# One transformer kernel on one core: ends of the walk merged, shifted copies moved to ScalarE, engine orders written anew

## The chip, the cores and the metric

The kernel runs on one core of a Trainium2 chip. The metric is the device time of that core in microseconds (us), from start to end of one execution, on fixed inputs. A core has five engines with a queue of instructions each: TensorE (PE, matrix products into eight PSUM banks), VectorE (DVE), ScalarE (ACT), GpSimd (POOL), and SyncE (SP), which here only issues DMAs. The queues run side by side; semaphores are all that orders them against each other, and inside a queue everything runs in the order in which it was written.

## The reference, cut to what matters

The input is `x`, 8 batches of 512 tokens of width 128, fp32. Everything after the input is done per batch, and no batch needs another.

```python
xn = layernorm(x)
x  = x + delta_rule_attention(xn)      # 4 heads of 128 / 32, a recurrence over the 512 tokens
       + local_stack(xn)               # 2 layers: windowed attention, then a gated MLP
xn = layernorm(x)
x  = x + latent_attention(xn)          # 16 heads of 8, causal softmax over all 512 keys
       + mixture_of_experts(xn)        # 6 experts, top 2 of 6, and a shared one

def shift_token(t):                    # used twice in each layer of local_stack
    t1, t2 = split(t, 2, axis=-1)
    t2 = pad(t2, one row in front)[:, :-1]
    return concatenate([t1, t2], axis=-1)

def layer(x):                          # of local_stack
    h = shift_token(x); q, k, v = split(h @ wqkv, 3)
    q = rotary(l2norm(q) * qs); k = rotary(l2norm(k) * ks)
    x = x + attention_in_windows_of_64_with_one_back(q, k, v) @ wo
    h = layernorm(shift_token(x)) * lg + lb
    a, g = split(h @ w1 + b1, 2)
    return x + (a * gelu(g)) @ w2 + b2
```

## The kernel before, in words

The weights stay in SBUF. A batch's tokens are four chunks of 128. Between the layers of the local stack the activations lie transposed, channels on partitions and tokens along the free axis (`xnT`, `hT`, `r1T`, `h2T`), so that `shift_token` is two copies: partitions 0 to 63 as they are, partitions 64 to 127 one column to the right (`shifted`, L1405 to L1407, run by DVE). It is called at `hcopy` (head norm to `hT`, the input of layer 0), at `fres` of both layers (`r1T` to `h2T`, before the MLP's layer norm, with a memset of the first column), and at the end of `fw2` of layer 0 (to `hT`, the input of layer 1). `hT_` (L1421) copies the transposed head norm from PSUM to `xnT`, on DVE as well.

The work of a batch is cut into seven streams of steps, one letter each. `f`: head norm, and the chunks' q, k, v products, rotation (`fqk`), norm (`frs`, `fscale`) and transposes (`fqT`, `fkT`). `b`: for each layer and chunk scores (`fS`), softmax (`fnorm`), transposes (`fPT`), values (`fPV`), output product (`fwo`); then the MLP (`fres`, `fln`, `fapply`, `hnT`, `fg`, `gelu`, `fa`, `fw2`); at the end `x1`, which adds the three parts, its layer norm (`x1_apply`), and its transposes (`xn2T`). `e`: the delta rule's keys, their gram blocks (`gram`), and `solve`, which inverts 16 x 16 diagonal blocks in 15 pairs of dependent DVE instructions, after the gram blocks have gone to DRAM and the diagonal has come back. `d`: the delta rule itself, a block inversion (`inv_v`, `inv_zx`) and a recurrence over chunks (`seq_*`), ending in `delta_back`, `delta_norm` and `oT0`. `m`: latent attention's projections (`lat`, `mq`, `rope`, `split`, `left`, `send`) and the experts (`eu`, `ew`, `e_down`). `a`: the pass that finds the maxima of the scores (`mS`, `mrow`). `c`: the pass with exponentials and values (`mST`, `mPV`, `matg`), ending in `aT` and `final`, which writes the batch out.

`walk` (L278) writes each engine's queue. It goes over periods; in period p there are `f`, `b` and `d` of batch p, `e` of batch p+1, and `m`, `a`, `c` of batch p-1. Period -1 holds only the head, two chunks of `f` and `e` of batch 0, and period 8 only `m`, `a`, `c` of batch 7. Inside a period each engine takes one step of the stream that the next letter of its string in `ORDER` names:

```python
    for p in range(-1, BATCH + 1):
        left = {s: collections.deque(x for x in steps if x[0] in parts) for s, steps in period(p).items()}
        for s in ORDER[engine][0 if p < 0 else 1 if p == 0 else p - BATCH + 4 if p >= BATCH - 1 else 2]:
            if left[s]:
                name, *at = left[s].popleft()
                parts[name](*at)
```

So there are five strings per engine: for period -1, 0, 1 to 6 (the steady one), 7 and 8. Nothing of a period can be written into a queue before all of the period ahead of it has been. The strings are data: they fix every order among steps that no dependency fixes. In the steady one, DVE's `solve` stands between the MLP's last gated product (`fa`) and `fw2` of layer 1.

Of the kernel before, what the change touches and what calls it, by code (L numbers as in the profile page):

```python
# [42 lines left out]
         "fefefeefeffffefeeeeeee"),  # L43
        (
         "bdfdfdddfbfdbbddbdfddbddfddfbbfbddbdddfdfdbdddffdbdebdbddbddbddddddddddbddbdbdbbddddbdbdbbbbbdbffdfeffefeffefb"
         "effbebebefbfffebeefebbfbebfbffbffbbbbfffbbfbfbbbbbbbbfbbbb"),
        (
         "dddddmbdmfddfbddbmbfddbffddbdfdddfdbdbfdbfdfmdbdddmdbdmdfdmfbddmdbbdbeddbddmddmddbmbdddmdbdmdbddbmddmdbmbbbabb"
         "abmabmafafmaaffaafmdfaffamabmafafmcabcbfcabfacbccfamacfcabacmcafcmafacbbcmcabcfabccaefaceacbceacafcafbcabecabc"
         "aeccabcfacbceacfccafeabcaeacbecfaccabaebcfcaecabccfcafcfcececcbccbcbbbbbcccbcccccccbccccb"),  # L50
        (
         "dddddmbdmfddfmbdbdfddbfbddfdbdfdfddddmbdbdfdbdddmdbdmdfddmddddfmfdbddmddfdmbdbdbdbdbdmddbdbmbdmbdmdbmmabmababb"
         "abmababdabmafamfafaaffamfacffacmacbcamccafafcbabmbcafccabcamccaffcmbcamacffaccbbacbcfcfcacabcafabcfafccabcabac"
         "bcabacbccaacabcabcabccabacaccbcaccacccbcbbcbbbbcbccbcccccbccccccccc"),
# [1964 lines left out]
```

## Time and profile before

| | |
|---|---|
| three runs, median (lowest to highest) | 2007.26 us (2005.38 to 2016.96) |
| the profiled execution's own time | 2011.66 us |
| its span, first to last instruction | 2009.9 us |
| instructions | 43996 |
| granted TensorE clock, mean | 0.949 of full |
| busy: PE, DVE, ACT, POOL | 1749.7, 1344.0, 938.6, 816.9 us |

Busy time is the time in which an engine had at least one instruction under way; issuing DMAs and waiting on semaphores is not counted. An engine's idle time is named after what released it. Line numbers are those of the kernel before. The clock is given as the share of full speed that was granted: 1.00 is 2.4 GHz, 0.50 is 1.2 GHz, and a value between is a mean over both. Where PE runs at 0.50, its instructions take up to twice as long and count as busy all the same.

### The profile page before, as it was taken

Reading aid. Unit: us, or ns where it says so; the run is one execution under the profiler, and the core shown is the slowest. Engines: PE = TensorE matmul, PEld = TensorE weight load, DVE = VectorE, ACT = ScalarE, POOL = GpSimd, SP = SyncE. Lnnn points to the kernel's source line nnn. Section 1 sums busy time; section 2 is a strip of 40 time slices with the busy share of each in tenths; the row PEclk is TensorE's granted clock in tenths of the full one; section 3 lists DMA queues with packets and bytes.
Section 4 is the critical chain, followed back from the end, with each engine's and each line's share of the span. In section 5 each row is a group of like instructions: output and inputs, shape, how many; then the busy total and the mean of one; then the engine's idle time right before and its main releaser. Section 6 shows DMA issues by size and latency. Waiting matters only on the chain.

```text
span 2009.9 us, 43996 instructions
## 1 busy us (share of the span) xinstructions
PE 1749.7 (87%) x16664; PEld 1136.1 (57%) x16664; DVE 1344.0 (67%) x3602; ACT 938.6 (47%) x2473; POOL 816.9 (41%) x819
## 2 busy tenths in 40 slices
PE   2597769998899979999899979999899989988787
PEld 1474537655674647655575647656575646745343
DVE  2464547776777767776678767787677766675373
ACT  1243434375434745366344745356443754345323
POOL 2434635364335625265235534175145534253000
PEclk9699889999899999999899999999899999999787
DMA  4210112201112022201122012201122011210020
GB/s 178 63 31 12 32 40 62 54 13 38 43 55 60 11 48 74 58 18 38 36 62 60 10 38 70 73 17 36 38 62 60 10 38 51 64 29 15 13 74 6
DMA packets 126625, 89.91 MB, mean 45 GB/s; under 512 B 42168, under 2 KB 113976, under 8 KB 126136
## 3 DMA queue, kind: packets, MB, share of 16 engines
q1 hardware_dynamic: 126128, 86.44, 16.0%
q8 instruction: 133, 2.18, 0.4%
q10 hardware_dynamic: 288, 0.67, 0.1%
q14 instruction: 76, 0.62, 0.1%
HBM read 46.84 MB, written 25.17 MB: 36 GB/s over the span
## 4 chain that ended last, share of the span: by engine, by line
PE 51%; DVE 16%; issue 8%; POOL 8%; ACT 6%; DVEq 0%; ACTq 0%; POOLq 0%
PE bank L691 7%; PE bank L1083 3%; PE bank L1069 3%; ACT shared L1333 2%; PE bank L798 2%; PE bank L832 2%; PE bank L824 2%; PE bank L1068 2%; PE bank L837 2%; PE bank L808 2%; POOL qk_rs L1790 2%; PE bank L1041 2%; PE bank L721 2%; POOL soft L1829 2%; DVE rot L1450 2%
## 5 line engine op out<-in xcount | busy, mean ns | idle before, releaser
L1829 POOL TENSOR_TENSOR soft<-soft,prec 128x512 f32<-128x512 f32 x128 | 137.3, 1082 | 442.4 <-DVE prec L1468 442.4
L1333 ACT ACTIVATE shared<-bank 128x512 f32<-128x512 f32 (+1 forms) x384 | 201.1, 528 | 240.5 <-PE bank L1069 238.8
L1637 DVE TENSOR_REDUCE nmx<-bank 128x1 f32<-128x512 f32 (+3 forms) x352 | 223.2, 637 | 128.2 <-PE bank L1041 125.8
L1243 ACT ACTIVATE soft<-bank,nmax 128x128 f32<-128x128 f32 x512 | 180.1, 382 | 101.4 <-DVE nmax L1460 100.5
L1790 POOL TENSOR_TENSOR qk_rs<-qk_rs,minus_half 128x16 f32<-128x16 f32 x64 | 187.7, 2932 | 5.3
L721 PE MATMUL bank<-w_sb,hT 128*128 128x512 f32 x256 | 138.0, 625 | 11.8 <-DVE hT L1407 6.0
L1068 PE MATMUL bank<-b_sb 128*128 128x128 bf16 x512 | 115.5, 227 | 34.7 <-ACT shared L1333 34.3
L1069 PE MATMUL bank<-shared 75*128 75x384 bf16 (+3 forms) x512 | 144.7, 310 | 0.0
L1788 POOL TENSOR_SCALAR rs_f<-mv_f 128x4 f32<-128x4 f32 x24 | 5.7, 236 | 325.8 <-DVE mv_f L1396 325.8
L1041 PE MATMUL bank<-shared 72*128 72x256 bf16 (+3 forms) x512 | 127.1, 300 | 0.0
L691 PE MATMUL bank<-c_sb,soft 128*128 128x128 f32 x608 | 100.1, 291 | 26.5 <-DVE soft L1402 12.9
L1207 ACT ACTIVATE rot<-bank 128x512 f32<-128x512 f32 x128 | 78.8, 616 | 92.1 <-PE bank L721 91.8
L1243 ACT ACTIVATION_READ_ACCUMULATOR soft<-bank,nmax 128x1 f32 x512 | 113.5, 222 | 0.0
L1068 PEld LDWEIGHTS bank<-b_sb 128*128 128x128 bf16 x512 | 49.2, 99 | 109.4 <-ACT shared L1333 74.5
L1252 ACT ACTIVATE soft<-bank 128x512 f32<-128x512 f32 x128 | 77.7, 608 | 69.7 <-PE bank L691 69.1
L1083 PE MATMUL bank<-shared,vaug 128*32 128x512 f32 (+3 forms) x1024 | 94.5, 466 | 9.8 <-ACT shared L1333 9.7
L1038 PE MATMUL bank<-b_sb 128*128 128x128 bf16 (+2 forms) x352 | 86.6, 246 | 17.2 <-DVE nmx L1637 15.0
L691 PEld LDWEIGHTS bank<-c_sb,soft 128*128 128x128 f32 x608 | 70.8, 148 | 53.9 <-POOL soft L1829 29.4
L1460 DVE TENSOR_REDUCE nmax<-bank 128x4 f32<-128x512 f32 x128 | 82.2, 683 | 28.1 <-PE bank L778 27.6
L1443 DVE TENSOR_REDUCE qk_ss<-rot 128x8 f32<-128x512 f32 x128 | 86.5, 676 | 11.0 <-ACT rot L1207 10.6
L727 PE MATMUL bank<-w_sb,hT 128*128 128x512 f32 x128 | 69.2, 623 | 15.7 <-DVE rot L1450 15.7
L1806 POOL TENSOR_TENSOR k_f<-k_f,rot 128x256 f32<-128x256 f32 x64 | 48.5, 757 | 70.4 <-DVE rot L1450 70.3
(250 smaller groups left out, 4503.0 us busy)
## 6 DMA issues: line engine op xcount, KB each, us to landing
shared<-parts_dram SPq DMA_DIRECT2D x64, 288.0 KB
vm<-v_f SPq DMA_DIRECT2D x112, 128.0 KB, 2.4
parts_dram<-parts SPq DMA_DIRECT2D x96, 128.0 KB, 2.4
L_dram<-the SPq DMA_DIRECT2D x32, 256.0 KB, 2.3
shared<-X_dram SPq DMA_DIRECT2D x32, 256.0 KB, 3.1
shared<-L_dram SPq DMA_DIRECT2D x32, 256.0 KB, 3.8
w_sb<-weights SPq DMA_DIRECT2D x1, 4167.0 KB, 19.4
x_tm<-x SPq DMA_DIRECT2D x8, 256.0 KB, 5.2
```

Of the source, the lines that this page charges most:

```text
L691: m = nc.tensor.transpose(ps[0:width, i * P:(i + 1) * P], src(i), ident)
L721: mm(place(("fq", "fk")[i], c)[:], hT[:, c * P:(c + 1) * P], W(f"wqkv{l}")[:, i * T:(i + 1) * T], start=True, stop=True).then_inc(fk_psum ...
L1038: mm(ps[:, :, c * P:w], B("identb"), repeat(B("causal"), len(heads)), start=True, stop=False, skip_group_check=True)
L1041: m = mm(ps[:, i], Qst[0:9 * DM, h * T + c * P:h * T + w], Kst[0:9 * DM, h * T:h * T + w], start=False, stop=True, skip_group_check=True)
L1068: mm(ps[:, at:at + P], B("identb"), B("causalT"), start=w == 0, stop=False, skip_group_check=True)
L1069: m = mm(ps[:, at:at + wide], Kst[0:9 * DM + 3, h * T + j * P:h * T + (j + 1) * P], Qst[0:9 * DM + 3, h * T + j * P:(h + 1) * T], start=Fa ...
L1083: m = mm(place("mPV")[VW * i:VW * (i + 1), j * P:T], vaug[:, at_v:at_v + VW], v4(PTm, 2, GROUP)[:, n % 2, i, at:at + wide], start=j == 0, ...
L1243: a = af(v4(p_sb, 2, 4)[:, j, g], place("fS", j)[:, g * P:(g + 1) * P], ACT.Exp, bias=nmax[:, at:at + 1], accum_out=psums[:, at:at + 1])
L1333: af(v4(PTm, 2, GROUP)[:, u % 2, i, 0:n], place("mST", b, i)[:, 0:n], ACT.Exp).then_inc(mexp_done, 1)
L1637: reduce(v3(nmx[:], HM)[:, h:h + len(heads), c], v3(place("mS", b, t)[:, 0:len(heads) * (c + 1) * P], len(heads)), AX, ALU.max, negate=Tru ...
L1790: return tt(dst, dst, minus_half[:, 0:dst.shape[1]], ALU.pow)
L1829: tt(p, p, spread(prec[:, at:at + NPAIR], P), ALU.mult).then_inc(fnorm_done, 1)
```

## The change

Three edits. First, periods -1 and 0 become one, and so do 7 and 8: `period(0)` is the old one of -1 with that of 0 behind it, stream by stream, `period(7)` likewise. There are now four strings per engine: for period 0, 1 to 5, 6, and 7. Steps of either old part may be written between steps of the other, as far as one stream's order allows. Second, `hT_`, `hcopy`, `shifted`, and with it the copies of `fres` and of `fw2` of layer 0, are run by ACT. DVE keeps the memset in `fres` and signals it separately, so that PE's `fln` waits for two signals per layer (one by DVE, one by ACT). Third, all strings are new. The computation is the same.

```diff
@@ period, walk
 def period(p):
 
+    if p == 0 or p == LAST:
+        one, two = (part(q) for q in ((-1, 0) if p == 0 else (LAST, BATCH)))
+        return {s: one[s] + two[s] for s in STREAMS}
+    return part(p)
+
+
+def part(p):
+
     if p < 0:
...
-    for p in range(-1, BATCH + 1):
+    for p in range(BATCH):
         left = {s: collections.deque(x for x in steps if x[0] in parts) for s, steps in period(p).items()}
-        for s in ORDER[engine][0 if p < 0 else 1 if p == 0 else p - BATCH + 4 if p >= BATCH - 1 else 2]:
+        for s in ORDER[engine][0 if p == 0 else p - BATCH + 4 if p >= BATCH - 2 else 1]:
@@ TensorE
                 def fln(b, l):
-                    pe.wait_ge(h2_done, ly(b, l) + 1)
+                    pe.wait_ge(h2_done, 2 * ly(b, l) + 2)
@@ ScalarE
+                def shifted(dst, src):
+                    af(dst[0:64, :], src[0:64, :], ACT.Copy)
+                    return af(dst[64:P, 1:T], src[64:P, 0:T - 1], ACT.Copy)
+
+                def hT_(b):
+                    act.wait_ge(head_psum, b + 1)
+                    if b:
+                        act.wait_ge(P_psum, NT * b)
+                        act.wait_ge(r1_done, ch(b - 1, 1, 0))
+                    af(xnT[:], place("hT")[:], ACT.Copy).then_inc(head_copied, 1)
+
+                def hcopy(b):
+                    act.wait_ge(head_copied, b + 1)
+                    if b:
+                        act.wait_ge(fv_psum, ch(b, 0, 0))
+                    shifted(hT, xnT).then_inc(hT_copied, 1)
...
+                def fres(b, l):
+                    act.wait_ge(r1_done, ch(b, l, NT))
+                    if l:
+                        act.wait_ge(h_done, b + 1)
+                    elif b:
+                        act.wait_ge(x1_psum, b)
+                    shifted(h2T, r1T).then_inc(h2_done, 1)
+
+                def fw2(b, l):
+                    if l == 0:
+                        act.wait_ge(r_done, ly(b, l) + 1)
+                        act.wait_ge(fv_psum, ch(b, 1, 0))
+                        shifted(hT, r2T).then_inc(h_done, 1)
@@ VectorE (hT_, hcopy and shifted go)
                 def fres(b, l):
-                    dve.wait_ge(r1_done, ch(b, l, NT))
                     if l:
                         dve.wait_ge(h_done, b + 1)
                     elif b:
                         dve.wait_ge(x1_psum, b)
-                    nc.vector.memset(h2T[64:P, 0:1], 0.0)
-                    shifted(h2T, r1T).then_inc(h2_done, 1)
+                    nc.vector.memset(h2T[64:P, 0:1], 0.0).then_inc(h2_done, 1)
...
                     stt(r2T[:], place("fw2")[:], W(f"cols{l}")[:, 6:7], r1T[:], ALU.add, ALU.add).then_inc(r_done, 1)
-                    if l == 0:
-                        dve.wait_ge(r_done, ly(b, l) + 1)
-                        dve.wait_ge(fv_psum, ch(b, 1, 0))
-                        shifted(hT, r2T).then_inc(h_done, 1)
```

What the strings mean where the prediction speaks of them, written out as steps (batch, layer, chunk as numbers; `|` is where a period ended):

```text
DVE, start.   before: k.0.3, fqk.0.0.1, beta, gram.0, gram.1, gram.2, gram.3, solve.0 | fS.0.0.0, bg, fqk.0.0.2, fnorm ...
              after:  k.0.3, fqk.0.0.1, beta, bg, gram.0, gram.1, fS.0.0.0, gram.2, fnorm.0.0.0 (both), gram.3,
                      fqk.0.0.2 (both), fwo.0.0.0, solve.0, fS.0.0.1, fqk.0.0.3 ...
PE, start.    before: hT.0, k.0.0, fqk.0.0.0 ... kT.0 to kT.3, gram.0 to gram.3 | fS.0.0.0, qT.0.0 ... qT.0.3, bg, fv.0.0.2 ...
              after:  hT.0, k.0.0, qT.0.0, k.0.1, fqk.0.0.0 ... bg, kT.0 to kT.3, gram.0, fqT.0, fkT.0, gram.1, fS.0.0.0,
                      gram.2, fqk.0.0.2 (both), gram.3, fPT (both), fv.0.0.2, fPV, fwo.0.0.0, fqT.1, fkT.1, fqk.0.0.3 (both),
                      fS.0.0.1, fv.0.0.3, fPT.0.0.1 (both), fqT.2, then the first inv_v
ACT, start.   after:  hT.0, k.0.0, hcopy.0, qT.0.0, k.0.1, fqk.0.0.0 ...
SP, start.    before: ... gram.0.3, solve.0, fv.0.0.0, fv.0.0.1, keep.0 | x_load.1, inv_load.0.0 ...
              after:  ... gram.0.3, fv.0.0.1, solve.0, fv.0.0.2, keep.0, x_load.1, inv_load.0.0 ...
ACT, layer 0's MLP in the steady string.
              before: ... seq_u.3, seq_o.3, gelu, eu.3, delta_back, fqk.1.0 ... (oT0 after fkT.1.0)
              after:  ... seq_u.2, fres, seq_o.2, ... seq_u.3, seq_o.3, delta_back, hT (of the next batch), gelu, fw2, oT0, eu.3, fqk.1.0 ...
PE there.     after:  ... hnT, delta_back, ew.2, fg.0, fg.1, fg.2, fa.0, fa.1, mS, fa.2, e_down.2, mS, fw2, mS, oT0, eu.3, mS, fqk.1.0 ...
DVE, end of the steady string (layer 1's MLP).
              before: fa.0, fa.1, fa.2, solve, fw2, x1, matg.3, x1_apply, final
              after:  fa.0, fa.1, fa.2, matg.2, fw2, x1, solve, matg.3, x1_apply, final
PE there.     before: ... mST (group 3) ..., x1, mPV, matg.3, aT, final, xn2T | qT (four), bg, mq, fS ...
              after:  ... x1, mST (eight more, with two mPV), mPV, matg.3, aT, xn2T, final | fS, mq, fqk, qT ...
PE, join of the last batches.
              before: xn2T.7, mPV, mST (four), mPV, matg, aT, final.6 | lat.7, mq.7.0.0, mq.7.0.1, latT.7 ...
              after:  xn2T.7, mPV, mST, lat.7, mST, mq.7.0.0, mST, mq.7.0.1, mST, mPV, matg, aT, final.6, latT.7 ...
```

## Rows read from the trace of the kernel before

**Rows 1.** The page, part 1: busy time, share, instructions of each engine.
```profile
PE 1749.7 (87%) x16664; PEld 1136.1 (57%) x16664; DVE 1344.0 (67%) x3602; ACT 938.6 (47%) x2473; POOL 816.9 (41%) x819
```

**Rows 2.** Windows (from:to, length, busy per engine, clock, DMA), cut at each L1522.
```profile
34.16:285.21 251.05, 186.79 (x1655) 125.76 (x1655) 127.93 (x344) 95.44 (x262) 121.45 (x119) 0.86 0.14 35
...
971.14:1199.13 227.99, 210.25 (x2087) 137.76 (x2091) 167.57 (x449) 116.63 (x309) 101.99 (x101) 0.99 0.17 44
...
1656.42:1877.26 220.84, 196.62 (x1951) 128.24 (x1955) 142.19 (x369) 103.37 (x280) 78.45 (x79) 0.95 0.13 36
1877.26:2009.90 132.64, 102.64 (x592) 53.82 (x592) 65.61 (x180) 39.37 (x77) 2.53 (x4) 0.77 0.13 35
...
182.00:285.21 103.21, 74.47 (x514) 44.96 (x514) 53.63 (x132) 45.41 (x124) 69.08 (x68) 0.88 0.16 38
```

**Rows 3.** Instructions in order of time, 80 to 93 us; one group by shape.
```profile
80.01 0.27 DVE L1558 MEMSET blk<- 128x256 f32 x1 [5.98 <-DMA blk<-L_dram]
...
89.44 1.28 DVE L1460 TENSOR_REDUCE nmax<-bank 128x4 f32<-128x512 f32 x2
...
93.16 2.08 PE L727 MATMUL bank<-w_sb,hT 128*128 128x512 f32 x2 [11.80 <-DVE rot L1450]
...
L1450 DVE TENSOR_TENSOR rot<-bank,c_sb 128x512 f32<-128x512 f32 x64 | 43.4, 679 | 0.0
```

**Rows 4.** The moved copies on DVE (min/median/max ns; group: busy, mean ns).
```profile
L1426 DVE COPY xnT<-bank x8: 680/692/693, 34.2 to 1515.6; 128x512 f32<-128x512 f32 x8
...
L1406 DVE COPY h2T<-r1T x16: 419/419/437, 160.9 to 1854.6; 64x512 f32<-64x512 f32 x16
...
L1407 DVE COPY h2T<-r1T 64x511 f32<-64x511 f32 x16 | 9.4, 589 | 0.2
```

**Rows 5.** Groups by shape on ACT: total busy, mean ns, idle before.
```profile
L1252 ACT ACTIVATE soft<-bank 128x512 f32<-128x512 f32 x128 | 77.7, 608 | 69.7 <-PE bank L691 69.1
...
L1333 ACT ACTIVATE shared<-bank 128x256 f32<-128x256 f32 x128 | 49.0, 386 | 78.6 <-PE bank L1069 78.4
...
L1262 ACT ACT_TABLE_LOAD x16 | 20.5, 1283 | 0.3
...
L1353 ACT ACTIVATE parts<-the 128x512 bf16<-128x512 f32 x16 | 10.8, 673 | 16.2 <-DVE the L1700 16.2
L1353 ACT ACTIVATE parts<-he 128x512 bf16<-128x512 f32 x16 | 10.5, 656 | 1.3 <-DVE he L1711 1.2
```

**Rows 6.** PE's waits, 971 to 1199 us: total, times, longest.
```profile
PE bank L1068 <- ACT shared L1333: 4.1, 8, 0.8
PE bank L824 <- ACT soft L1266: 2.0, 1, 2.0
PE bank L1038 <- DVE nmx L1637: 1.8, 3, 0.9
...
PE bank L721 <- DVE hT L1407: 0.6, 1, 0.6
```

**Rows 7.** Instructions in order of time, end of that interval.
```profile
1187.62 2.79 PE L837 MATMUL bank<-soft,w_sb 128*128 128x512 f32 x6
...
1195.37 0.74 DVE L1512 SCALAR_TENSOR_TENSOR h2T<-bank,w_sb,r1T 128x512 f32<-128x512 f32 x1
...
1202.63 2.57 DVE L1402 TENSOR_SCALAR soft<-x_tm,mv_f,rs_f 128x128 f32<-128x128 f32 x4 [0.34 <-POOL rs_f L1790]
```

**Rows 8.** PE's waits in the ramp, 34 to 285 us.
```profile
PE bank L691 <- DVE soft L1402: 5.3, 2, 4.2
PE bank L691 <- POOL shared L1861: 2.8, 1, 2.8
```

**Rows 9.** Instructions in order of time, join of the last batches; one window.
```profile
1897.81 1.77 PE L1134 MATMUL bank<-w_sb,xn2T 128*128 128x38 f32 x8
1898.12 0.69 DVE L1668 TENSOR_TENSOR at_tm<-bank,acc 128x512 f32<-128x512 f32 x1 [5.81 <-PE bank L1102]
1899.38 3.76 PE L1125 MATMUL bank<-xn2T,w_sb 128*128 128x512 f32 x4
...
1896.00:1903.00 7.00, 7.00 (x22) 4.53 (x21) 2.25 (x10) 0.00 (x0) 1.27 (x2) 0.50 0.12 37
```

More of the change, by code:

```diff
@@ new lines @@
+         "ddddffdfffddffffbffdbebebebeffebfffebbbebeffebeefbbebebfbffbbbbfbffffbfbbbbbbbbb"),
+        (
+         "bmfddfbdbddbmbddmddfddffdfbddmfddmbbddmbddbdmdmdffdddfbdmdfmdbdebddbddbddmdfdbddmddbddbdbdbdmdbddmddbdmbbbbbab"
+         "mabadmafafmaaffamaffamafafmbamfacfamcbabcfcabccabcamfacmcfaccabcafcmafcacbbfccabcmacbceaccaecaffaceacbccaeaffa"
+         "bcabcebcabcabcceacfafabcaeacbaeccbecabcaeacbfaccecfcfcbecfbccbcbebffbcbcbccbcccccccccccbc"),
+        (
+         "bdfmdfbdbddbmdbdmddffdfdfddbdfmddmbbddmbddbdmdfmdfddfdbdmdfmdbdebddbddmddbdfdbddmddbdmbddbdbdbdddmddbmdbbbbbab"
+         "mabadmafafamaffamfafaamffambamfacfamcabbcfacbccabcamacfmcafcacbcfacmabcafcbfcacbcmacbcaeccaecaffaceacbcaecaffa"
+         "cbabcebcabcabccaecfafabcaeacbaeccbecabcaeacbfaccecfcfcbecfbccbbcbbebcffcbccbcccccccccccbc"),
@@ new lines @@
+         "ebbeeebbfbbebbfbffbbbbbbbb"),
+        (
+         "bmbbffdmedbdmddmddmmmdbddbmbddmfdmdddbdmefdmmddmbmbdddbmdddbdddmdbdbdmbdddddbdbmbddbmbmddbababmbaamafafamafama"
+         "famambamabbafaafamabmamaabababfmafamacaaaabeeaebababaaeababacbaabaafafeababeababefbefbebbcbbecbc"),
+        (
+         "bbbmffddmedddmmbdddmmmbddbmbddmfdmdddbdemfmdmddmbmbddbddmddddbdmdbdbdmbdddddbdbmbddbmbdmdbabbmabaamafafamafama"
+         "famambamabbafamfaaambaamabababfmacamafaaeaeababababaeeaababacebaabaafafabbaeababefbcebfbebbbecbc"),
@@ L1372, in eu @@
                     af(cols(the, n % 2, T), place("eu", b)[:], ACT.Tanh, scale=0.5).then_inc(eth_done, 1)
-                walk("ACT", {"fqk": fqk, "fv": fv, "fqT": fqT, "fkT": fkT, "fS": fS, "fPT": fPT, "fPV": fPV, "gelu": gelu, "xn2T": xn2T_,
+                walk("ACT", {"hT": hT_, "hcopy": hcopy, "fres": fres, "fw2": fw2, "fqk": fqk, "fv": fv, "fqT": fqT, "fkT": fkT, "fS": fS, "fPT": fPT, "fPV": fPV, "gelu": gelu, "xn2T": xn2T_,
                              "k": k, "beta": beta_, "bg": bg, "kT": kT_, "qT": qT_, "inv_v": inv_v, "seq_u": seq_u, "seq_o": seq_o, "seq_s": seq_s,
@@ L1419, in happly @@
                     apply("h", v3(hn_tm, NT), v3(cols(x_tm, b % 2, T), NT), head_root, b + 1, head_norm_done)
-                def hT_(b):
-                    dve.wait_ge(head_psum, b + 1)
-                    if b:
-                        dve.wait_ge(P_psum, NT * b)
-                        dve.wait_ge(r1_done, ch(b - 1, 1, 0))
-                    nc.vector.tensor_copy(xnT[:], place("hT")[:]).then_inc(head_copied, 1)
-                def hcopy(b):
-                    dve.wait_ge(head_copied, b + 1)
-                    if b:
-                        dve.wait_ge(fv_psum, ch(b, 0, 0))
-                    shifted(hT, xnT).then_inc(hT_copied, 1)
                 def fqk(b, l, c, i):
@@ L1771, in e_down @@
                     m.then_inc(ey_done, 1)
-                walk("DVE", {"hln": hln, "happly": happly, "hT": hT_, "hcopy": hcopy, "fqk": fqk, "fS": fS, "fnorm": fnorm, "fwo": fwo, "fres": fres,
+                walk("DVE", {"hln": hln, "happly": happly, "fqk": fqk, "fS": fS, "fnorm": fnorm, "fwo": fwo, "fres": fres,
                              "fln": fln, "fapply": fapply, "hnT": hnT_, "fa": fa, "fw2": fw2, "x1": x1, "x1_apply": x1_apply,
```

71 lines of the change are left out of this document (26 added, 45 removed).

## The prediction

> **What bounds the kernel now.** I read the page first, then a table of engine time by stage, then the waits and the instructions in order of time where a stage shows idle time on TensorE (PE).
>
> The page gives PE 87% of the span, against 67% for VectorE (DVE), 47% for ScalarE (ACT) and 41% for GpSimd (POOL) [rows 1]. That is a mean over unlike stages. The stages are cut at the start of the add that ends each batch's layer stack (L1522) [rows 2]. Span less PE busy is PE's idle time: ramp (34 to 285 us) 251.1 - 186.8 = 64.3 us; a steady interval 228.0 - 210.3 = 17.7 us, 8%; the interval that leads to the last batch 24.2 us; the tail 132.6 - 102.6 = 30.0 us. So PE bounds the steady intervals, and a new order can win there at most a part of 17.7 us, six times; the ramp is bound by waits and holds the largest sum of idle time in one place.
>
> In the ramp, one wait of 11.8 us stands out [rows 3]: DVE has nothing for 6.0 us until the diagonal blocks are back from DRAM at 80.0, and then runs the 31 small steps of `solve` until 89.4. The score maxima of chunk 0 and the work on chunk 2 stand behind `solve` in DVE's queue, and PE waits from 81.4 to 93.2 for the second's rotation product.
>
> **The change part by part.**
>
> *Copies from DVE to ACT.* Per batch: the head copy (L1426), and a pair of copies at `hcopy`, at both `fres` and at `fw2` of layer 0; 9 of 9 copies leave DVE, the memset stays. On DVE [rows 4] the head copy takes 0.69 us, a half copy 0.42; the second half at `fres` has a mean of 0.589 us, so some of the 16 were stretched. Relief per batch: 0.69 + 4 x 0.42 + 2 x 0.424 + 2 x 0.589 = 4.4 us, 35 us in all. ACT has no fp32 SBUF-to-SBUF copy in the trace. Its nearest rows [rows 5] are 512 columns from SBUF to bf16, 0.66 to 0.67 us, and 512 columns from PSUM, 0.60; as a lower bound, 256 columns cost 0.39. I take 0.63 us, by the rows of the same width: a pair costs 1.26 us where DVE needs 0.85, 0.4 us more latency (ends: -0.1 and +0.5), and ACT takes on 0.6 + 8 x 0.63 = 5.6 us per batch. It has 228 - 116.6 = 111 us free in a steady interval [rows 2], so its load is covered, but not its queue: the `fw2` pair waits for DVE's sum, and with it the attention projection's copy, an expert's tanh and the next squares behind it on ACT; the PE steps placed there (a score step, a transpose, an expert product, a score step) cover some 3 us.
> The Trainium skill (ScalarE: Activation LUTs, Rules for kernel authors) speaks against this edit: it gives simple elementwise work to VectorE. By that rule three exposed pairs would lose 3 x 0.4 us in each of 8 batches, 10 us; by the rows, the only exposed one now is `fw2`'s, where PE waits 0.6 us for DVE's copy [rows 6], so 8 x 0.4 = 3 us at most. The skill's GPSIMD Engine Reference (Specifications) has the two-port DVE copies share an SBUF interface with POOL; the stretched mean agrees, and what the rule would free, 16 x 0.17 = 2.7 us of DVE, is already in the relief.
> What DVE's relief is worth: PE's waits on DVE in one steady interval are nmx 1.8, hT 0.6, and 3.4 in seven smaller ones of 0.2 to 0.9, 5.8 us [rows 6]. At best all go, at worst none; I take a quarter, -1.5 us per interval, as most sit directly behind a DVE result and not behind its queue.
>
> *Steady orders.* Two places can be priced. (a) In layer 0, `delta_back` and the head copy now come ahead of the GELU in ACT's queue: 0.6 x 3 = 1.8 us more before the table load of 1.3 us [rows 5], with two gate products on PE to cover it, 0.9 us each by the down product's 2.8 for three pairs [rows 7]. PE has no such wait there now; I take +1.4 us (ends 0 and 3). In layer 1 an exp moves from before to behind the load, so that the present wait of 2.0 us [rows 6] falls to some 1.2: -0.8. (b) `solve` moves behind `fw2` and `x1`. Now it holds the stack's sum from 1190.4, when the down product ends, to 1195.4 [rows 7]; after, the sum and `x1` come about 5 us earlier, but `solve` (9 us) then stands ahead of the last head group's division and `x1_apply`. Eight exp steps of about 1 us each are the cover. Walked through: x1 ends near 1195, `solve` near 1204, the division and apply near 1207.5, where now apply ends at 1205.2, and the last output product then follows the transposes instead of covering the wait for them. I take +0.5 us, as the stack's own start moves forward too, between -3 (the earlier sum carries through) and +4 (all of it shows). Sum of an interval: -1.5 + 1.4 - 0.8 + 0.5 = -0.4 us, six times -2.4; the ends, each term at its own, are -6 and +6 per interval.
>
> *Ramp.* The merged order puts chunk 0's maxima, its sums, chunk 2's rotation and the first residual tile (1.3 + 0.3 + 6 x 0.68 + 0.3 = 6.0 us of DVE [rows 3]) ahead of `solve`, into the 6 us in which it waits for its load. PE gets the rest of chunk 0, all of chunk 3's first products and chunk 1's scores before the first step of the block inversion, some 10 us of matmuls, most of the 11.8. Against it: fewer grams follow each other (five steps come between), so `solve` starts some 3 us later, and the delta stream with it; the head copies on ACT stand behind `k`'s copies and start the front stream about 2 us later. The queries' four products and `bg` move ahead of it, to where PE waits anyway. SyncE's queue has a V shift (two DMA issues) ahead of the block load; it is issued while DVE still works on chunk 2. Later in the ramp the front and layer streams, not delta, set x1, and the idle time after 182 us [rows 2] stays with `solve` of batch 1 again in front of a residual tile. Sum: -11.8 + 3 (solve) + 2 (head) - 2 (part of two waits, 4.2 us for a layer norm and 2.8 for the delta norm [rows 8]) = -9 us. Ends: -20 (three more such waits go) and +5 (delta's lateness carries through).
>
> *Last batches.* The penultimate interval loses its boundary only on paper; -1 us (ends -5, +5). At the join, the latent and query products (1897.8 to 1903.1, at the lower clock level) move in among the last exp steps, where PE waits 0.5 to 0.7 us for each; the rope then waits only for the final add (1898.1 now) [rows 9]. That add comes 1 to 3 us later for the products put ahead of it; the second rope term starts near 1901.5 instead of 1903.2: -2 us (ends -8, if the clock, 0.5 in this stretch [rows 9], stays up, and +3).
>
> Sum: -9 - 2.4 - 1 - 2 = -14 us. The profiled execution took 2011.7 us (span 2009.9 and 1.8 around it), so 1997 on its footing; it stands 4.4 us above the median of three, 2007.3, so **1993 us** against that.
>
> **The rivals.**
> *A, the forecast:* ends gain 10 to 20 us, steady intervals stand still; 1985 to 2000.
> *B, steady orders gain too:* DVE's relief empties PE's waits on it and the earlier `x1` carries through, -3 us in each of six: 1993 - 18 = 1975. For it: DVE at 168 of 228 us and 5.8 us of waits on it. Against it: most of the 17.7 us are chains of 0.5 to 0.7 us behind single ACT results, which no relief of DVE touches.
> *C, slower:* `solve` in its new place delays `x1_apply`, and every batch's transposes, by more than the cover. Its place is the end of each interval; its price is up to 5 us there plus 1.4 at layer 0's GELU, six times; with -3 to -14 from the ends that gives 2010 to 2038. It decides once PE's idle time between the end of the `x1` products and the next batch's first scores passes about 5 us.
> *D, the ends give nothing:* the hole is filled, but delta is late by 3 us and the work moved forward leaves the later ramp as idle as before; 2005. For it: the layer stream is a chain of latencies, with 29 us idle after 182 us (103.2 - 74.5) [rows 2] and nothing left over to fill it. Against it: that stream itself starts 15 us ahead.
>
> **How the numbers follow.** A 0.45, B 0.25, D 0.16, C 0.14. The likeliest, A, gives 1993. To hold 8 in 10, the range reaches down to 1972 (most of B) and up to 2016 (D, the lower part of C). Faster by over 1% (below 1987): B and a quarter of A, 0.36. Slower by over 1% (above 2027; 1% is about what a measurement of this kernel can tell from none): the upper two thirds of C, 0.10. Within: 0.54.
>
> **What would show it.** The hole before the second V product of the ramp shrinks from 11.8 to under 4 us, and the first x1 add starts near 276 us instead of 285.2. A steady interval stays at 227 to 229 us; if it is below 226, B. The copy pairs on ACT take 1.2 to 1.35 us; if 0.8, the price of the move is gone. PE's wait for the GELU shows in layer 0 as 1 to 2 us. C shows as idle PE ahead of the last group's transposes, behind the division on DVE. From the last x1 add to the end: 132.6 us now, 130 after. I am wrong if the steady intervals move by more than 3 us each, since six of them weigh more than both ends.

## The result, and the profile after

The changed kernel takes 1984.0 us (median of 4 runs, 1975.1 to 1990.0) where the kernel before, run beside it, takes 2008.7: a ratio of 0.9863, 95% interval 0.983 to 0.9896 (the two medians alone would give 0.9877). The forecast was 1993 in a range of 1972 to 2016. All ratios leave out the executions in a slower state, of which there were two, both of `e6_hole` below. The profiled execution, at 1975.1 us (span 1973.3), was the fastest of the four, and a second profile of the same kernel (below, as `after_again`) has a span of 1980.0, so what one profile shows must be read with care.

The page's first part, against [rows 1]: DVE has 72 instructions less and ACT 72 more, 23 us less and 40 us more.

```profile
PE 1736.5 (88%) x16664; PEld 1127.2 (57%) x16664; DVE 1321.1 (67%) x3530; ACT 978.3 (50%) x2545; POOL 814.9 (41%) x819
```

The windows of the changed kernel, cut as [rows 2] at the start of each x1 add (L1534 here): ramp, a steady interval, the penultimate one, the tail, the late part of the ramp.

```profile
34.00:268.62 234.62, 183.32 (x1656) 119.62 (x1655) 125.83 (x332) 103.30 (x275) 118.97 (x117) 0.89 0.13 33
948.65:1174.35 225.70, 209.43 (x2085) 137.32 (x2083) 164.56 (x440) 121.55 (x318) 101.95 (x101) 0.97 0.17 45
1630.16:1847.20 217.04, 195.65 (x1987) 127.55 (x1988) 146.59 (x395) 110.97 (x295) 76.80 (x77) 0.96 0.15 39
1847.20:1973.30 126.10, 96.97 (x592) 50.84 (x591) 65.18 (x180) 38.83 (x77) 2.53 (x4) 0.83 0.13 37
182.00:268.62 86.62, 65.65 (x458) 39.09 (x457) 44.65 (x115) 43.42 (x120) 56.67 (x56) 0.86 0.12 27
```

Subtract PE's busy time from the length and two different savings come apart. Over the span the profile is 36.6 us shorter: 23.4 us of PE's idle time (260.2 to 236.8, span less busy) and 13.2 us of its busy time (1749.7 to 1736.5), although the matmuls are the same 16664. Idle time by stage, now less before: ramp 51.3 - 64.3 = -13.0; first interval -3.1; the next five -1.5, -1.7, -1.5, -0.9 and +2.0 (the last has an order of its own); penultimate 21.4 - 24.2 = -2.8; tail 29.1 - 30.0 = -0.9. The tail is 6.5 us shorter, and 5.7 of them are busy time, at a granted clock of 0.83 where [rows 2] has 0.77.

The hole of [rows 3], in order of time: the instruction of DVE that starts `solve`, and the matmul behind the hole.

```profile
77.73 0.27 DVE L1570 MEMSET blk<- 128x256 f32 x1
...
91.73 2.07 PE L731 MATMUL bank<-w_sb,hT 128*128 128x512 f32 x2 [9.76 <-DVE rot L1468]
```

`solve` starts 2.3 us earlier than before, not 3 later, and the hole is still 9.8 us: it did not close. It moved on by one chunk. Chunk 2's rotations now run ahead of `solve`, and PE stands before the rotation product of chunk 3, whose rotations are behind it.

PE's waits in a steady interval (total, times, longest), against [rows 6], and the moved copies by shape on ACT, against [rows 4]:

```profile
PE bank L1072 <- ACT shared L1368: 3.3, 6, 0.7
PE bank L828 <- ACT soft L1301: 3.0, 2, 1.7
PE bank L1042 <- DVE nmx L1649: 1.4, 2, 1.3
PE bank L695 <- DVE at_tm L1674: 1.4, 1, 1.4
...
PE bank L725 <- ACT hT L1206: 0.2, 1, 0.2
```

```profile
L1206 ACT ACTIVATE h2T<-r1T 64x511 f32<-64x511 f32 x16 | 10.0, 626 | 0.2
...
L1205 ACT ACTIVATE hT<-h2T 64x512 f32<-64x512 f32 x8 | 5.0, 629 | 40.9 <-DVE h2T L1528 40.9
...
L1214 ACT ACTIVATE xnT<-bank 128x512 f32<-128x512 f32 x8 | 4.8, 601 | 8.3 <-PE bank L695 6.6 <-PE bank L981 1.7
```

A half copy takes 0.63 us and the head copy 0.60, as forecast. ACT stands 40.9 us in all before the `fw2` pairs, and PE does not notice (0.2 us per interval for that result).

### The profile page after: what moved, and what is told of

It is laid out like the page before. It is cut to its first block, busy times and chain, and to the rows that moved or that the text cites. A ratio compares the mean times of both kernels' runs of the same rounds, so it can differ in the third digit from the quotient of the medians.

```text
span 1973.3 us, 43996 instructions
## 1 busy us (share of the span) xinstructions
PE 1736.5 (88%) x16664; PEld 1127.2 (57%) x16664; DVE 1321.1 (67%) x3530; ACT 978.3 (50%) x2545; POOL 814.9 (41%) x819
## 3 DMA queue, kind: packets, MB, share of 16 engines
q1 hardware_dynamic: 126128, 86.44, 16.3%
## 4 chain that ended last, share of the span: by engine, by line
PE 59%; DVE 20%; issue 7%; ACT 6%; POOL 6%; DMA 0%; SPq 0%; DVEq 0%; POOLq 0%; ACTq 0%
PE bank L695 8%; PE bank L1087 3%; PE bank L802 3%; PE bank L812 3%; PE bank L1073 2%; DVE blk L1574 2%; PE bank L782 2%; PE bank L836 2%; PE bank L725 2%; PE bank L1045 2%; PE bank L841 2%; PE bank L1184 2%; DVE nmx L1649 2%; PE bank L1164 2%; PE bank L989 2%
## 5 line engine op out<-in xcount | busy, mean ns | idle before, releaser
L1841 POOL TENSOR_TENSOR soft<-soft,prec 128x512 f32<-128x512 f32 x128 | 132.3, 1039 | 453.4 <-DVE prec L1486 452.7
L1072 PE MATMUL bank<-b_sb 128*128 128x128 bf16 x512 | 115.5, 227 | 25.6 <-ACT shared L1368 24.3
L1818 POOL TENSOR_TENSOR q_f<-q_f,rot 128x256 f32<-128x256 f32 x64 | 46.3, 724 | 179.6 <-DVE rot L1468 179.6
L695 PE MATMUL bank<-c_sb,soft 128*128 128x128 f32 x608 | 100.3, 295 | 18.0 <-DVE soft L1437 8.8
L1087 PE MATMUL bank<-shared,vaug 128*32 128x512 f32 (+3 forms) x1024 | 96.4, 475 | 13.7 <-ACT shared L1368 13.5
L1461 DVE TENSOR_REDUCE qk_ss<-rot 128x8 f32<-128x512 f32 x128 | 86.9, 679 | 25.2 <-ACT rot L1228 23.4
L731 PE MATMUL bank<-w_sb,hT 128*128 128x512 f32 x128 | 73.5, 657 | 17.3 <-DVE rot L1468 16.9
```

Of the source, the lines that this page charges most:

```text
L695: m = nc.tensor.transpose(ps[0:width, i * P:(i + 1) * P], src(i), ident)
L1072: mm(ps[:, at:at + P], B("identb"), B("causalT"), start=w == 0, stop=False, skip_group_check=True)
L1087: m = mm(place("mPV")[VW * i:VW * (i + 1), j * P:T], vaug[:, at_v:at_v + VW], v4(PTm, 2, GROUP)[:, n % 2, i, at:at + wide], start=j == 0, ...
L1818: tt(d[:, :, 0:h], d[:, :, 0:h], r[:, :, h:DF], ALU.add)
L1841: tt(p, p, spread(prec[:, at:at + NPAIR], P), ALU.mult).then_inc(fnorm_done, 1)
```

## The experiments

Eleven more kernels ran, and the changed one once again. An order string names for each step of an engine the stream that it is drawn from, so a kernel can mix the old and new strings of single periods. This table holds what they gave: the ratio to the kernel before with its interval; PE's idle time over the span (span less busy); then length / idle time of PE by stage in the profile. "Steady" is the interval that leads to the fifth batch's add, as in [rows 2].

| kernel | ratio (95%) | idle | ramp | first | steady | penult. | tail |
|---|---|---|---|---|---|---|---|
| before | 1 | 260.2 | 251.1/64.3 | 228.8/20.0 | 228.0/17.7 | 220.8/24.2 | 132.6/30.0 |
| changed | 0.9863 (.983-.990) | 236.8 | 234.6/51.3 | 226.4/16.9 | 225.7/16.3 | 217.0/21.4 | 126.1/29.1 |
| after_again | 0.9849 (.981-.989) | 239.2 | 238.6/51.0 | 226.5/17.1 | 225.9/16.5 | 216.6/21.8 | 125.8/29.5 |
| e1_copies | 1.0044 (1.003-1.006) | 265.5 | 252.5/63.6 | 228.9/20.8 | 230.2/18.5 | 222.6/25.6 | 132.2/30.0 |
| e2_orders | 0.9913 (.989-.994) | 254.7 | 239.5/53.4 | 220.1/18.4 | 228.9/19.5 | 221.8/20.9 | 130.0/29.4 |
| e3_start | 0.9965 (.994-.999) | 254.6 | 242.2/51.9 | 230.2/22.2 | 227.4/18.5 | 220.9/25.5 | 132.0/30.1 |
| e4_steady | 1.0011 (1.000-1.003) | 257.5 | 254.8/64.5 | 217.2/16.6 | 227.5/16.5 | 234.2/28.2 | 131.0/30.1 |
| e11_end | 0.9944 (.992-.997) | 245.4 | 232.8/52.8 | 219.6/16.6 | 225.7/16.3 | 234.4/28.1 | 131.3/29.9 |
| e5_solve | 1.0239 (1.021-1.027) | 302.4 | 236.0/53.1 | 236.1/29.2 | 239.5/27.3 | 218.5/20.4 | 130.1/29.3 |
| e6_hole | 0.9920 (.988-.996) | 247.7 | 248.9/59.6 | 222.5/17.5 | 228.2/16.0 | 216.6/21.8 | 125.9/29.5 |
| e7_gelu | 0.9897 (.987-.992) | 246.6 | 240.3/52.7 | 221.2/18.2 | 229.1/17.8 | 217.1/21.5 | 126.1/29.1 |
| e8_early | 0.9843 (.982-.986) | 236.0 | 239.5/52.0 | 226.4/17.0 | 225.7/16.2 | 216.4/21.0 | 125.8/29.6 |
| e9_fw2 | 0.9878 (.984-.992) | 241.6 | 245.2/50.2 | 219.3/18.4 | 227.4/17.9 | 216.3/21.6 | 125.9/29.5 |
| e10_six | 0.9868 (.984-.989) | 234.8 | 236.9/53.3 | 218.0/16.9 | 226.3/17.8 | 232.0/19.8 | 126.9/28.9 |

**Copies or orders.** Two kernels make one edit each. `e1_copies` keeps the old strings, with the copies placed in ACT's queue where the trace has DVE do them:

```diff
 DVE:  - hT, hcopy steps
       - shifted(h2T, r1T) in fres; shifted(hT, r2T) in fw2
 ACT:  + fres, hT of the next batch   (ahead of the third expert's tanh)
       + fw2                          (ahead of layer 1's first projection copy)
       + hcopy of the next batch      (behind fkT of chunk 2, layer 1)
```

> The kernel before with only the copies moved to ScalarE: every engine keeps the order of the kernel before (the 9 copies of a batch stand on ACT where DVE did them, by time). Theory 1 (the orders made the gain, the copies are near neutral): a copy pair costs 1.25 us where DVE needed 0.85, exposed at fw2 of layer 0, 0.4 us in each of 8 batches, so 2010 to 2015 us against 2009 for the kernel before; a steady interval 228 to 228.6 us, the ramp (to the first x1 add) still near 285. Theory 2 (the 4.4 us of DVE that each batch is relieved of made the gain): 1990 to 2000 us, a steady interval near 226.5 us, and PE's waits on DVE (5.8 us per steady interval) cut by 2 us or more.

`e2_orders` is the reverse: the old code of the copies on DVE, under the new strings.

```diff
 ACT:  - hT, hcopy, fres, fw2 steps
 DVE:  + hT of the next batch ahead of delta_sum; hcopy ahead of matg of group 1
       + the copies in fres and fw2
```

> The changed kernel's orders with the copies given back to DVE. Theory 1 (orders): within 5 us of the changed kernel, 1980 to 1990 us, ramp near 269 us, steady interval 225.5 to 227. Theory 2 (relief of DVE): 4.4 us per batch come back on DVE, of which the intervals show 1.5 or more each, so 1996 to 2008 us. A third reading, that the new orders were made for copies on ACT and need them there: slower than the kernel before, over 2010.

The copies alone cost 0.44%, 9 us; the orders alone give 0.87%, 17 us; both give 1.4 to 1.5%, 27 to 30 us. So the same nine copies lose 9 us under the old orders and win some 10 under the new ones (there the two intervals just touch; PE's idle time, 254.7 us against 236.8 and 239.2, says the same). Neither theory had that, and the waits tell why. PE's waits in a steady interval of `e1_copies`, then of `e2_orders`:

```profile
PE bank L1074 <- ACT shared L1370: 4.9, 8, 1.0
PE bank L830 <- ACT soft L1303: 2.0, 1, 2.0
PE bank L1044 <- DVE nmx L1651: 1.8, 3, 0.9
PE bank L727 <- ACT hT L1208: 1.0, 1, 1.0
PE bank L697 <- DVE at_tm L1676: 0.9, 1, 0.9
```

```profile
PE bank L1072 <- ACT shared L1337: 3.5, 6, 0.8
PE bank L695 <- DVE at_tm L1666: 2.7, 1, 2.7
...
PE bank L1042 <- DVE nmx L1641: 2.2, 3, 1.1
...
PE bank L725 <- DVE hT L1411: 1.1, 1, 1.1
```

Under the old orders DVE is relieved of 4.3 us per interval (167.6 to 163.3 busy) and PE's two longest waits on it stay what they were, 1.8 and 0.9 us: what PE waited for was a result, not DVE's queue. The price shows: the exp steps wait 4.9 us instead of 4.1, the sum's copy 1.0 instead of 0.6. Other waits got shorter, so that 0.8 of these 1.2 us are left as idle time per interval, and 5.3 us over the span (265.5 against 260.2). Under the new orders DVE's queue is tight where PE reads from it: with the copies on DVE the final add is 2.7 us late, the row maxima 2.2 and the copy 1.1; on ACT 1.4, 1.4 and 0.2, and an interval has 16.3 us of idle time in place of 19.5. The Trainium skill (ScalarE: Activation LUTs, Rules for kernel authors) gives `relu`, `max`, `min`, `add` and `mul` to VectorE; the prediction took that to hold for copies too and made a loss of 10 us of it, from three exposed pairs per batch. `e1_copies` lost 9, but at other places than these pairs, and `e2_orders` against the changed kernel shows the opposite sign, so for these copies such a rule holds or fails with the order of the queues. (Where the copies stand in these two kernels was chosen here; other places would move the figures.)

Idle time is not the whole of it. The orders alone make the time 17 us shorter, but PE's idle time only 5.5 us (260.2 to 254.7). The page of `e2_orders`:

```profile
PE 1735.1 (87%) x16664; PEld 1126.0 (57%) x16664; DVE 1353.3 (68%) x3602; ACT 937.8 (47%) x2473; POOL 817.1 (41%) x819
```

PE is busy for 14.6 us less than in the kernel before, with the same matmuls and the same mean granted clock (0.949), and the two profiled executions, 1991.6 and 2011.7 us, stand at their kernels' medians (1991.4 and 2011.3). So two thirds or more of what the orders alone gave lie in PE's busy time, on average 1.8 us in each of the five intervals behind the first. Why is not shown.

**Stage by stage.** Copies on ACT throughout; the new strings for the start alone, for the steady periods alone, and for all but the last period.

```diff
 for p in range(BATCH):
-    ORDER[engine][new strings of all periods]
+    e3_start:  new in period 0;       old in 1 to 7
+    e4_steady: new in 1 to 6;         old in 0 and 7
+    e11_end:   new in 0 to 6;         old in 7
```

> Copies on ACT, the new merged order for the start alone (period 0); steady periods and the end keep the order of the kernel before. Theory 1: the ramp's 16 us are the start order's own: first x1 add at 268 to 271 us, steady intervals as in the kernel before (228 to 229), total 1993 to 1998. Rival: what the start gives is lent by the next period (its work stands later) and is paid back in the second interval: ramp near 270 but second interval 235 or more, total 2003 or more.

> Copies on ACT, the new orders for the six steady periods alone; start and end as in the kernel before. Theory 1 (each stage's gain is that of its own order): ramp near 285 us, steady intervals 225.5 to 227, penultimate and tail as before (220.8 and 132.6), total 1998 to 2003. Theory 2 (the steady gain is DVE's relief, not the order): the same intervals as the kernel with only the copies moved, within 0.5 us.

> The changed kernel with the order of the kernel before in its last period alone (periods 7 and 8 joined), start and steady new. Theory 1 (the stages' gains are separate; the end is worth the prediction's 3 us plus what the profile shows, 4 to 10): penultimate 221, tail 130 to 132.6, total 1988 to 1994. Rival (the steady orders leave work over that only the new end takes in, as the 234 us before the last add in the kernel with new steady orders alone hint): penultimate 230 or more, total 1998 to 2005.

The start gives 0.8% against `e1_copies`, 16 us, and little of its 12 us of idle time is paid back (1.4 us in the first interval); the median of 2005.6 us is still above the 1998 of theory 1, although the second interval of its rival, 235 us or more, did not come (230.2). The steady strings then give 0.2% (`e3_start` to `e11_end`), 4 us, and the end 0.8 to 1.0%, some 17 us. The step of 0.2% is within the intervals, though the idle time fell by 9 us. `e4_steady`, the steady strings alone, gives 0.3% against `e1_copies`; neither of its theories had that, for both left the penultimate interval as it was, and it took 234 us. The 17 us are far more than the end's own order. Behind the new steady strings the old last period takes 234 us, with 28 us idle, where the new one takes 217 with 21. The penultimate interval of `e11_end`:

```profile
1625.38:1859.73 234.35, 206.27 (x1987) 133.49 (x1988) 146.61 (x395) 111.42 (x295) 76.42 (x77) 0.92 0.13 36
```

PE's waits of the penultimate interval, `e11_end` and then the changed kernel:

```profile
PE bank L1074 <- ACT shared L1370: 8.0, 13, 1.3
PE bank L1044 <- DVE nmx L1651: 2.8, 5, 1.1
```

```profile
PE bank L1072 <- ACT shared L1368: 4.4, 8, 0.7
PE bank L1042 <- DVE nmx L1649: 2.6, 3, 1.3
```

13 exp steps stand bare instead of 8. The steady order hands its border on in another state, and the end that was made with it takes that in. The rival of `e11_end`'s expectation was right. But the waits explain less than half: of the 17 us between the two intervals 6.7 are idle time and 10.6 are PE's busy time (206.3 against 195.7 for the same 1987 matmuls), at a granted clock of 0.92 against 0.96. `e4_steady` has both figures again (28.2 us idle, 0.92), so this is no accident of one profile; why the clock is lower there is open. The new end behind the old steady strings was not run.

**The same order, profiled again.**

> The changed kernel once more, for a second profile. In its first profile the ramp took 268.6 us and the tail 126.1; kernels with the same start or the same end order took 276.2 and 273.5 (start) and 130.0 (end), with the granted clock at 0.50 in other places. Theory 1 (the rest is where the clock falls): this profile shows a ramp of 270 to 277 us or a tail of 129 to 131, with steady intervals unchanged at 225.5 to 228; total 1980 to 1988. Rival (the ramp of 268.6 is the order's own): 268 to 269.5 and 126 again.

Windows: the ramp of `after_again`; the ramp of `e3_start` and 24 us of it; the same 24 us of the changed kernel's first profile; the ramp of `e11_end`. All four have the same strings in period 0.

```profile
34.00:272.60 238.60, 187.57 (x1657) 123.73 (x1655) 125.83 (x332) 103.27 (x275) 119.08 (x117) 0.86 0.13 32
```

```profile
34.00:276.16 242.16, 190.29 (x1656) 126.82 (x1655) 125.90 (x331) 103.33 (x275) 118.93 (x117) 0.86 0.14 36
110.00:134.00 24.00, 22.51 (x179) 19.44 (x179) 7.93 (x23) 6.61 (x24) 3.09 (x4) 0.57 0.18 50
```

```profile
110.00:134.00 24.00, 21.36 (x310) 18.07 (x310) 9.34 (x30) 10.65 (x35) 4.29 (x5) 1.00 0.19 51
```

```profile
34.00:266.82 232.82, 180.06 (x1657) 116.84 (x1655) 125.68 (x331) 103.28 (x275) 119.07 (x117) 0.90 0.13 33
```

Same matmuls, idle time 51.0 to 52.8 us, and lengths from 232.8 to 242.2: the 10 us between them are PE's busy time, 180.1 to 190.3. In one profile the engine ran 110 to 134 us at 0.57 of its clock, mostly at the lower level (1.2 GHz), and got through 179 matmuls where another profile has 1.00 and 310. So the idle time of the ramp belongs to the order, to within 2 to 3 us, and the length is that plus where the clock fell. Theory 1 held for the ramp (272.6 us), though one steady interval, 230.2 us, lay outside its range, and not for the tail: 125.8 to 126.9 us in seven profiles with the new end, but 130.0 and 130.1 in two others with it (`e2_orders`, `e5_solve`), with the same 29 us of idle time.

**The hole and `solve`.** `e6_hole` lets chunk 1's maxima and chunk 3's rotations go ahead of `solve` in DVE's queue, `e8_early` puts `solve` one step further forward.

```diff
 DVE, period 0:
-  fwo.0 | solve.0 | fS.1  fqk.3.0  fnorm.1.0  fnorm.1.1  fqk.3.1
+  fwo.0 | fS.1  fqk.3.0  fnorm.1.0  fnorm.1.1  fqk.3.1 | solve.0     (e6_hole)
+  solve.0 | fwo.0 | fS.1  fqk.3.0  fnorm.1.0  fnorm.1.1  fqk.3.1     (e8_early)
```

> The changed kernel with solve of batch 0 moved behind chunk 1's maxima and chunk 3's rotations on DVE (some 6 us of DVE work come ahead of it), so that the 9.8 us hole of PE before chunk 3's rotation product closes. Theory 1 (the prediction's: idle PE in the hole is on the path of the ramp): the hole shrinks to under 3 us and the ramp is 3 to 6 us shorter. Rival (the ramp is bound by solve and the inversion behind it, the hole only shows it): the idle time moves behind solve, to the first steps of the inversion, and the ramp is 0 to 6 us longer. The first x1 add has to be read beside the clock, which moved it by 7 us between two profiles of this order.

> The changed kernel with solve of batch 0 one step further forward on DVE, ahead of the first residual tile, for which DVE waits 3 us (72.5 to 75.5) while the diagonal blocks' load, issued at 71.5, should be back near 74. Theory from the closed hole (the ramp is bound by solve and the inversion loads behind it): solve starts 1 to 2 us earlier, the inversion's first product too, and the ramp is 1 to 3 us shorter; total 1980 to 1983. Rival (PE's work on the residual tile's bank or the output product behind it is what is late): the 9 us residual tile delay stalls PE instead, ramp 2 us longer or more.

PE's two stalls in `e6_hole`, in order of time:

```profile
83.23 2.08 PE L731 MATMUL bank<-w_sb,hT 128*128 128x512 f32 x2 [3.20 <-DVE rot L1468]
...
101.75 1.11 PE L695 MATMUL bank<-c_sb,shared 128*128 128x128 f32 x4 [14.57 <-DMA shared<-X_dram]
```

The hole closed from 9.8 to 3.2 us, and 14.6 us opened behind it, before the first product of the block inversion: idle time 59.6 us in the ramp, 8 more. The rival holds. (Its ten runs spread from 1982 to 2022 us: four of up to 1991 us have a mean granted clock of 0.941 to 0.944, six of 2001 us and more one of 0.919 to 0.930. What sets it off is open.) The hole only shows where PE runs out of work that does not need `solve`; to fill it at `solve`'s expense moves it. `e8_early` did start `solve` at 74.1, where the two profiles of the changed kernel have 77.7 and 75.8, yet the ramp's idle time stayed at 52.0 and the ratio is within the interval of the changed kernel. Its two stalls in place of the one:

```profile
84.94 1.01 PE L768 MATMUL bank<-b_sb 128*128 128x512 bf16 x2 [6.41 <-issue]
...
91.07 2.07 PE L731 MATMUL bank<-w_sb,hT 128*128 128x512 f32 x2 [3.20 <-DVE rot L1468]
```

The first product of the inversion starts at 95.5 us, where the two profiles of the changed kernel have 95.7 and 94.2: its theory fell, and an earlier `solve` alone no longer brings the inversion forward. No kernel here beats the changed one by more than the intervals.

**`solve` behind the sum.** Undone in the steady periods:

```diff
 DVE, periods 1 to 6:
-  ... fw2.1  x1  solve  matg.3  x1_apply
+  ... solve  fw2.1  x1  matg.3  x1_apply
```

> The changed kernel with solve of the next batch moved back ahead of the stack's sum and the x1 add on DVE, in the six steady periods. Theory 1 (the new place is worth what the walk-through gave, about nothing: sum and x1 5 us earlier, division and apply 2 us later): steady intervals within 1 us of 226.3, total 1980 to 1990; PE's wait of 1.4 us for the final add (at_tm) goes, a wait for x1_apply's transposes or for the sum comes. Rival C of the prediction (solve behind x1 delays x1_apply): undoing it gains 2 us or more per interval, total below 1975. Opposite (the earlier sum is where the steady gain of 2 us comes from): intervals at 228 or more, total 1993 to 2000.

Waits of PE and then DVE's instructions at the end of that interval in `e5_solve`:

```profile
PE bank L849 <- DVE h2T L1528: 11.4, 1, 11.4
```

```profile
1209.55 0.27 DVE L1570 MEMSET blk<- 128x256 f32 x1 [3.92 <-DMA blk<-L_dram]
...
1218.98 0.74 DVE L1528 SCALAR_TENSOR_TENSOR h2T<-bank,w_sb,r1T 128x512 f32<-128x512 f32 x1
```

The interval is 13.8 us longer, 11.0 of them idle time. In the new order the grams come so late that the blocks are not back when the sum is due: DVE idles 3.9 us for them, solves for 9.4, and PE waits 11.4 for the sum. The move was not a detail worth half a microsecond either way; it is what lets the grams be late. None of the three theories had this size; the third, that the earlier sum is worth something, had the sign.

**Layer 0's GELU ahead of `delta_back`.**

```diff
 ACT, periods 1 to 6:
-  ... delta_back  hT  gelu.0  fw2.0 ...
+  ... gelu.0  delta_back  hT  fw2.0 ...
```

> The changed kernel with layer 0's GELU put ahead of delta_back and the next head copy on ACT, in the six steady periods, as the kernel before had it. Theory 1 (the prediction's +1.4 us per interval): PE's wait for the GELU falls from 3.0 us in two to 1.7 in one, intervals 1 to 1.4 us shorter, total 6 to 8 us lower than the changed kernel. Rival (covered by other work): the wait moves to oT0's transposes or to the head's products, intervals within 0.5 us.

PE's waits in its steady interval:

```profile
PE bank L836 <- DVE soft L1524: 2.5, 1, 2.5
PE bank L828 <- ACT soft L1301: 1.7, 1, 1.7
```

The GELU wait fell from 3.0 to 1.7 us as expected, and a new one of 2.5 took its place: `delta_back`'s copies now come 106.3 us behind the x1 add instead of 100.3, `delta_sum` waits for them at the head of DVE's queue, and the activation's own product behind it. Idle time is 1.6 us more in this interval and 7 to 10 us more over the span; the time is 0.3 to 0.5% longer, which is within the intervals. Both theories were wrong: the wait moved, as the rival had it, but to another place, and it grew.

**Two small ones.** `e9_fw2` gives the `fw2` pair back to DVE, `e10_six` runs period 6 by the steady string.

```diff
 e9_fw2:   DVE fw2: + tensor_copy x2 behind the sum;  ACT: - fw2 steps
 e10_six:  ORDER[engine][2] = ORDER[engine][1]
```

> The changed kernel with the copy pair behind the stack's sum of layer 0 (fw2) back on DVE, the other seven copies of a batch on ACT. By the prediction's term (ACT's pair 0.4 us slower than DVE's, exposed at fw2 alone): up to 0.4 us per batch gained, 1980 to 1983 us. Rival (DVE's relief is what the new orders live on, 10 us in all between the copies on DVE and on ACT): a quarter of that or more lost, 1985 to 1988, with the final add's wait on PE (1.4 us per interval) growing by the 0.85 us that DVE takes on.

> The changed kernel with period 6 by the steady string instead of one of its own. Its own string makes that interval 229.8 us where steady ones take 226, and leads to a penultimate interval of 217. Theory 1 (the 4 us are lent: work brought forward for the last period): interval 226, penultimate 221, total unchanged within 3 us. Rival (the string of its own is just worse): total 3 to 4 us lower.

`e9_fw2` is inconclusive in time (its interval covers that of the changed kernel); idle time rose by 2.4 to 4.8 us, which speaks for its rival. In its steady interval PE waits for the final add and the maxima as long as in `e2_orders`, so this one pair is enough to make DVE late there:

```profile
PE bank L695 <- DVE at_tm L1673: 2.6, 1, 2.6
PE bank L1042 <- DVE nmx L1648: 2.2, 3, 1.1
```

`e10_six` left the total where it was: the interval of period 6 had 15.9 us idle instead of 19.7, the penultimate one 19.8 instead of 21.4, but this ran 36 us at a clock of 0.53 and took 232 us. Whether its 2 to 4 us of idle time are real gain stays open.

## Why the prediction was right, and where it was wrong

The range held and the direction was right, but the gain of 14 us in the sum was 10 too small, and two of its steps were right for other reasons than given. Most of the chance, 0.54, stood on a change of under 1%; the measured 1984 us lies between the likeliest rival, A, and B: a gain of over 1%, to which it gave 0.36. Two of its bounds do not follow from their terms: the lower end of a steady interval adds up to -9.6 us, not -6, and rival C reaches up to 2043 us, not 2038. Neither moved the forecast.

- *Copies.* 0.63 and 0.60 us each: right, and so was the relief, 4.3 us per interval under the old orders and 4.0 under the new (4.4 forecast). On the page DVE lost only 23 us of the 35, since the new orders by themselves add 9 to its busy time (1344.0 to 1353.3 in `e2_orders`). What the relief is worth, a quarter of 5.8 us whatever the order, is the step that failed: nothing under the old orders, 3.2 us of idle time per interval under the new ones. DVE's slack has no price of its own; it has one in a given queue order.
- *Steady orders.* Forecast -0.4 us per interval, measured -1.5 of idle time and -2.3 of length in the interval shown; over all six -6.7 and -9.7 us, where -2.4 was forecast. Of its terms, layer 0's GELU wait came as forecast (1.3 of the 1.4 us); layer 1's fell by 0.3 instead of 0.8; the final add waits 0.5 us more, as forecast for `solve`'s new place. What was missed are small waits that vanished, 1.6 us on POOL, 0.8 and 0.7 on single ACT results, and others that came: 0.8 for `kTf`, 0.7 more at the exps ahead of L1087, 1.3 more for rotations. By the prediction's own sign, an interval below 226 us (225.7), this was rival B. It had twice the size, and its mechanism only in part: the relief counts under the new orders, but PE's waits on DVE are not emptied, 6.1 us in all where they were 5.8. C was ruled out: PE's wait for the late final add is 1.4 us, and undoing the move cost 11 us of idle time (`e5_solve`).
- *Ramp.* Forecast -9; idle time -13.0, in every profile with the new start 11 to 14 us below before (save `e6_hole`). But "most of the 11.8" did not close: the hole gave 2, and closing it costs 8 more. The idle time went at other places: 5.9 us before 100 us (the hole's 2 among them; the grams no longer follow each other, and in the whole ramp PE waits for their results 1.4 us in one wait, where it was 5.4 in five), and 7.8 us after 182 us, which the prediction left standing, with "nothing left over to fill it". `solve` started 2.3 us early, not 3 late. So the hole's term of -11.8 was worth -2, and where the term of -2 stood for part of two late waits, the late ramp lost 7.8. The 2 us for the head copies were not measured by themselves. Rival D fell with the 13 us.
- *Last batches.* Forecast -1 and -2; idle time -2.8 and -0.9. The tail's other 5.7 us are busy time at a higher granted clock (0.83 against 0.77), which the prediction had as the end of its range, if the clock "stays up": so it was in seven of nine profiles with this order, and in none of five with the old one (131.0 to 132.6 us). But the edit was priced as if it stood alone. Behind the new steady orders it is worth 17 us, of which 6 to 9 are idle time (245.4 us in `e11_end` against 239.2 and 236.8).
- *The footing.* The two profiles lie 37 and 30 us below the one before, the medians 25 and 30 us below those of the kernel before beside them. A forecast of a few microseconds per stage can't be read off one profile's lengths.

## What to carry to other kernels

Compare orders by the bottleneck engine's idle time, stage by stage, before its length; it repeats to 1 to 3 us where the length moves by ten. But hold its sum against medians over several runs: of the 17 us that the orders alone gave here, idle time explains 5.5, and of the 17 us of the end 6 to 9. The rest is busy time that repeats as well. A stall names the work that ran out, not the chain that bounds: ask what would be late if the stalled engine had that work. And orders, queue loads and borders that were made together are priced together: here one edit cost 9 us or gave 10, depending on what stood beside it, and another, forecast by itself at 3 us, was worth 17 behind the orders it was made with.

## What the runs showed of the hardware

The granted clock falls in other places from profile to profile of the same strings. The changed kernel's first and second profile differ by 6.7 us in span: in the ramp 51.3 and 51.0 us idle, but 183.3 and 187.6 busy; in the second interval 225.5 and 230.2 us long, with 16.2 and 16.3 idle. In both profiles PE came out of the same hole of 9.7 to 9.8 us, and then the clock fell near 110 us in the second, to 0.73 on average from 110 to 134 us, while the first has 1.00 there:

```profile
110.00:134.00 24.00, 22.37 (x220) 19.52 (x220) 7.28 (x21) 8.53 (x30) 3.35 (x4) 0.73 0.17 51
```

Nothing in these traces tells what decides it. The runs of the changed kernel spread over twice this difference, 1975 to 1990 us. And the clock is not chance alone: the last interval ran at 0.77 to 0.79 in all five profiles with the old end, and at 0.81 to 0.83 in seven of nine with the new one.
